# A gated recurrence with a binarized FFN: u in two single-pass parts, gates spread over two sweeps, signs on ScalarE, W_out of block 0 inside the second sweep

## The reference

```python
u = x @ W_in + b_in
g = sigmoid(x @ W_gate + b_gate)
h_t = tanh(h_prev @ A + u_t @ Bm)          # step by step, h0 = 0
y_t = h_t @ C.T + u_t @ D.T
y_t = g_t * y_t + (1 - g_t) * x_t
x = layernorm(x + (ys @ W_out + b_out + x))
bw = mean(abs(w), axis=1) * sign(w)        # of w1 and of w2
h = gelu(x @ bw1.T + b1)                   # exact gelu
out = layernorm(x + (h @ bw2.T + b2))
```

## Time and profile before

| | us |
|---|---|
| median of 3 runs (lowest to highest) | 439.53 (438.86 to 439.70) |
| the profiled execution, its own time | 438.74 |
| its span, first to last instruction | 436.9 |
| TensorE matmul busy | 422.2 (97%) |
| VectorE busy | 361.3 (83%) |
| ScalarE busy | 309.8 (71%) |
| GpSimd busy | 305.9 (70%) |

### The profile page before, as it was taken

How to read it: one execution, slowest core, us unless ns; L and a number is a source line. 1 busy time by engine, 2 the same in 40 slices (tenths; PEclk the granted TensorE clock), 3 DMA queues, 4 the chain that set the end, 5 groups by cost and what they waited for, 6 DMA issues and landing times.

```text
span 436.9 us, 8056 instructions
## 1 busy us (share of the span) xinstructions
PE 422.2 (97%) x2691; PEld 305.2 (70%) x2691; DVE 361.3 (83%) x788; ACT 309.8 (71%) x570; POOL 305.9 (70%) x304
## 2 busy tenths in 40 slices
PE   7999999999999999999999999999999999999982
PEld 4787887777756777676776867768677676766651
DVE  2666777766466899999999999999999999998574
ACT  1222224655547878889898898988989889797781
POOL 5199722255479977797977979779797797673523
PEclk9999999999999999999999999999999999999997
DMA  7954460000110113435153451434514245151422
GB/s 226 360 151 133 141 144 2 2 0 2 48 51 0 50 48 50 78 69 98 48 98 115 71 108 48 98 104 56 132 48 98 96 54 143 48 98 49 50 98 96
DMA packets 43895, 37.17 MB, mean 85 GB/s; under 512 B 35505, under 2 KB 37297, under 8 KB 43857
## 3 DMA queue, kind: packets, MB, share of 16 engines
q1 hardware_dynamic: 42528, 35.66, 33.6%
q0 software_dynamic: 272, 0.66, 0.6%
q10 hardware_dynamic: 1056, 0.36, 0.3%
HBM read 19.90 MB, written 8.39 MB: 65 GB/s over the span
## 4 chain that ended last, share of the span: by engine, by line
PE 72%; DVE 16%; ACT 4%; issue 4%; DMA 1%; SPq 0%; POOL 0%; POOLq 0%; DVEq 0%; ACTq 0%
PE bank L1049 17%; PE bank L1037 14%; PE bank L925 10%; PE bank L881 8%; PE bank L793 7%; DVE hid L1393 7%; PE bank L786 6%; PE bank L896 3%; PE bank L867 3%; ACT hid L644 3%; PE bank L778 3%; DVE gT L1406 3%; DVE bank L1376 3%; DVE bank L1399 2%; DVE gT L1388 2%
## 5 line engine op out<-in xcount | busy, mean ns | idle before, releaser
L1037 PE MATMUL bank<-xT,w1s 128*128 128x512 f16 x512 | 126.9, 380 | 2.4 <-DVE hid L1393 1.7
L1049 PE MATMUL bank<-w2s,hid 128*128 128x256 f16 x1024 | 125.3, 273 | 0.9 <-DVE gT L1406 0.8
L1049 PEld LDWEIGHTS bank<-w2s,hid 128*128 128x128 f16 x1024 | 98.6, 98 | 31.4 <-issue 5.6
L636 ACT ACTIVATE bank<-bank,b_col,alpha 128x512 f32<-128x512 f32 x128 | 96.8, 756 | 15.3 <-PE bank L1037 14.9
L1393 DVE SCALAR_TENSOR_TENSOR hid<-bank,small,hid 128x512 f16<-128x512 f32 x128 | 94.6, 740 | 14.9 <-ACT hid L644 14.9
L644 ACT ACTIVATE hid<-bank,small 128x512 f16<-128x512 f32 x128 | 86.6, 692 | 19.0 <-PE bank L1049 17.8
L1037 PEld LDWEIGHTS bank<-xT,w1s 128*128 128x128 f16 x512 | 46.0, 98 | 48.0 <-DVE hid L1393 7.1
L410 POOL TENSOR_TENSOR ys_lo<-gT,ys_hi 128x512 fp32r<-128x512 f32 x30 | 38.3, 1278 | 24.8 <-ACT ys_hi L609 24.8
L793 PE MATMUL bank<-hu,w_rec 128*128 128x128 f32 x208 | 45.5, 300 | 1.1 <-DVE hu L1156 0.9
L405 POOL TENSOR_TENSOR gT<-gT,xT 128x512 f32<-128x512 f32 x30 | 38.3, 1276 | 11.2 <-DVE gT L1279 11.0
L426 POOL TENSOR_TENSOR gT<-x_rows,b_row 128x1024 f32<-128x1024 f32 x16 | 38.0, 2378 | 9.6 <-DMA xT<-gT 9.6
(11 more groups left out here) (145 smaller groups left out, 807.7 us busy)
## 6 DMA issues: line engine op xcount, KB each, us to landing
x_load<-in_L_attn_x SPq DMA_DIRECT2D x16, 512.0 KB, 3.6
gT<-in_L_attn_x SPq DMA_DIRECT2D x15, 512.0 KB, 3.8
out_rows<-gT SPq DMA_DIRECT2D x15, 512.0 KB, 3.4
gT<-in_L_ffn_w SPq DMA_DIRECT2D x2, 1024.0 KB, 11.4
gT<-in_L_attn_x SPq DMA_DIRECT2D x4, 128.0 KB, 2.8
out_rows<-gT SPq DMA_DIRECT2D x2, 256.0 KB, 2.1
xT<-gT SPq DMA_TRANSPOSE x28, 4.1
w_gate<-in_L_attn_W_gate ACTq DMA_DIRECT2D x1, 256.0 KB, 7.6
```

The source lines that it names most:

```text
L636: nc.scalar.activation(bank[which][:, :], bank[which][:, :], ACT.Gelu, bias=b1_col[:, c:c + 1], scale=alpha1[:, c:c + 1]).then_inc(s_gelu, 1)
L1037: done = nc.tensor.matmul(bank[which][:, :], w1s[:, c, k, :], x1T[:, n, :, part, :, k, :], start=(k == 0 and part == 0), stop=(k == KD - 1 ...
L1049: done = nc.tensor.matmul(bank[tile // 2][:, tile % 2 * DM:(tile % 2 + 1) * DM], hid[:, c % 3, part, tile * P:(tile + 1) * P], w2s[:, :, c ...
```

## The change

1. **u from parts.** From the fourth block on (in load order, o >= WHOLE_U = 3), u is no longer a whole fp32 product. `w_pack` holds the low part of W_in in its left 64 columns and the high part in its right 64 (made by GpSimd at the start). VectorE casts x to its high part (`x_high`), GpSimd subtracts the low part, and `u_part` multiplies w_pack with the high part and then the low part. The right half of the result plus the left half is u: ScalarE copies the left half out (`u_copy`, into `u_rest`), and VectorE adds it in `u_out`.
2. **Transposes** of two steps share a bank, and `x_out` copies two steps at once.
3. **Gates** of five blocks (order `GATE_ORDER`, places 0 to 4) use the parts of x that u has needed and run as single pieces beside the steps from 12 on: one piece a step up to step 56, two up to 59, three from 60. 14 blocks have gates by parts (165 of their 168 pieces stand in the sweeps); two blocks (13 and 14 in x, places 14 and 15) have whole products in the tail.
4. **Signs** of w1 and w2 are made by ScalarE with the Sign function in eight quarters after the tanh of steps 28, 32, 34, 38, 40, 44, 46 and 50. w1 and w2 are loaded one block later.
5. **Block 0**: y in steps 86 and 90 in place of 90 and 96; W_out of block 0 in steps 97 to 100, in banks 4 and 5, no gate pieces in these six steps.
6. **Tail**: the order of GpSimd, ScalarE and VectorE is new around blocks 0 and 1, and `out_products(1, 0)` stands behind `y_products(2, 1)`.

```diff
+    WHOLE_U = 3
+    BEFORE = 5
+    IN_PARTS = NB - 2
+    GATE_ORDER = (9, 12, 15, 2, 5, 0, 1, 6, 7, 8, 3, 4, 10, 11, 13, 14)
+    FIRST_Y = (WARM + 11 * STEPS + 2, WARM + 12 * STEPS + 2)
+    FIRST_OUT = WARM + L - 7
+    def pieces_at(t):
+        if t < WHOLE_U * STEPS or t in FIRST_Y or FIRST_OUT <= t < FIRST_OUT + STEPS:
+            return 0
+        return 1 if turned_at(t)[0] < NB + 1 and t < NB * STEPS - 7 else 2 if t < NB * STEPS - STEPS else 3
...
+            pool.wait_ge(s_win, 16)
+            pool.tensor_copy(w_pack[:, :, NS:P], w_in[:, :, NS:P]).then_inc(s_wp, 1)
+            pool.wait_ge(s_wp, 1)
+            pool.tensor_tensor(w_pack[:, :, 0:NS], w_in[:, :, NS:P], w_pack[:, :, NS:P].bitcast(F32),
+                               ALU.subtract).then_inc(s_wp, 1)
...
-            for i, (stage, negative, sign) in enumerate(((w1_stage, neg_w1, w1_sgn), (w2_stage, neg_w2, w2_sgn))):
-                pool.wait_ge(s_w12, 32)
-                pool.tensor_scalar(negative, stage, 0.0, None, ALU.is_lt).then_inc(s_neg, 1)
-                pool.tensor_scalar(sign, stage, 0.0, None, ALU.is_gt).then_inc(s_neg, 1)
-                pool.wait_ge(s_neg, i * 2 + 2)
-                pool.tensor_tensor(sign, sign, negative, ALU.subtract).then_inc(s_sgn, 1)
+            for o in range(WHOLE_U, NB):
+                high, low = parts_of(o)
+                j = (B0 + o) % NB
+                for half in range(2):
+                    at = slice(half * (N // 2), (half + 1) * (N // 2))
+                    pool.wait_ge(s_xph, (o - WHOLE_U) * 2 + half + 1)
+                    pool.tensor_tensor(low[:, :, at], xT[:, j, :, at], high[:, :, at].bitcast(F32),
+                                       ALU.subtract).then_inc(s_xpl, 1)
...
             hu_low(1, 0)
-            hu_low(1, 1)
             first_rstd(0, 0)
             pool.wait_ge(s_rs1, 1)
+            hu_low(1, 1)
+            first_rstd(0, 1)
+            mix(1, 0)
+            pool.wait_ge(s_ys, KD + 1)
             hu_low(2, 0)
-            mix(1, 0)
-            first_rstd(0, 1)
-            pool.wait_ge(s_rs1, 2)
+            mix(1, 1)
+            pool.wait_ge(s_ys, KD + 2)
             hu_low(2, 1)
-            mix(1, 1)
...
+            def u_copy(o, half):
+                act.wait_ge(s_umm, o * 2 + half + 1)
+                act.wait_ge(s_u, o * 2 + half)
+                nc.scalar.activation(u_rest[NS:P, :], bank[4 + half][0:NS, 0:N // 2], ACT.Copy).then_inc(s_uc, 1)
...
+            SIGN_STEPS = (28, 32, 34, 38, 40, 44, 46, 50)
+            for t in range(WARM + L):
...
+                if s % 2 == 1 and WHOLE_U <= o + 1 < NB:
+                    u_copy(o + 1, s // 2)
+                if t in SIGN_STEPS:
+                    sign_quarter(*divmod(SIGN_STEPS.index(t), 4))
+                for g in range(NB * KD):
+                    if gate_half_done(g) + 1 == t:
+                        gate(g // KD, g % KD)
...
+            gate(14, 0)
             act.wait_ge(s_done, 1)
             hu_high(1, 0)
             hu_high(1, 1)
-            gate(GATED, 1)
-            gate(GATED + 1, 0)
-            gate(GATED + 1, 1)
+            gate(14, 1)
+            gate(15, 0)
+            gate(15, 1)
+            nc.scalar.activation(small[0:1, 29:30], ident[0:1, 0:1], ACT.Gelu)
+            act.wait_ge(s_scale, 1)
             hu_high(2, 0)
             hu_high(2, 1)
...
             ys_high(1, 0)
-            gate(GATED + 3, 0)
+            x1_hi(0, 0)
             ys_high(1, 1)
-            gate(GATED + 3, 1)
-            x1_hi(0, 0)
-            gate(GATED + 4, 0)
             x1_hi(0, 1)
...
+            def u_part(o, half, part):
+                pe.wait_ge((s_xph, s_xpl)[part], (o - WHOLE_U) * 2 + half + 1)
+                for k in range(KD):
+                    done = nc.tensor.matmul(bank[4 + half][:, 0:N // 2], w_pack[:, k, :],
+                                            parts_of(o)[part][:, k, half * (N // 2):(half + 1) * (N // 2)],
+                                            start=(part == 0 and k == 0), stop=(part == 1 and k == KD - 1))
...
+            for t in range(WARM + L):
+                o, s = divmod(t, STEPS)
+                if s % 2 == 0 and o < NB:
+                    pe.wait_ge(s_u, o * 2 + s // 2 + 1)
+                pe.wait_ge(s_h, t + 1)
+                scan_step(T0 + t if t < WARM else t - WARM, s % 2, s_scan)
+                if t < 2 * STEPS:
+                    opening(t)
+                elif o + 1 < NB:
+                    if t == 2 * STEPS:
+                        pe.wait_ge(s_wp, 2)
+                    u_part(o + 1, s // 2, s % 2)
+                    if o + 2 < NB:
+                        transpose_step(o + 2, s)
+                if t == WHOLE_U * STEPS:
+                    pe.wait_ge(s_wgs, 2)
+                for i in range(pieces_before(t), pieces_before(t + 1)):
+                    gate_piece(i)
+                if t // STEPS == NB - B0 + PREP:
+                    prepare_rows(s)
+                for m in range(KD):
+                    if t == FIRST_Y[m]:
+                        y_products(0, m)
+                if FIRST_OUT <= t < FIRST_OUT + STEPS:
+                    if t == FIRST_OUT:
+                        pe.wait_ge(s_ylo, KD)
+                    out_of(0, t - FIRST_OUT)
...
+            for i in range(pieces_before(WARM + L), IN_PARTS * KD * 6):
+                gate_piece(i)
+            gate_half(14, 0)
             pe.wait_ge(s_cmp, 3)
+            nc.tensor.matmul(bank[2][0:1, 0:1], gap_flag, ones[0:NS, 0:1], start=True, stop=True).then_inc(s_cnt, 1)
+            gate_half(14, 1)
...
+            gate_half(15, 0)
+            gate_half(15, 1)
             y_products(1, 0)
             y_products(1, 1)
...
             hidden(0, 0)
             hidden(0, 1)
             y_products(2, 1)
+            out_products(1, 0)
             out_products(1, 1)
             hidden(0, 2)
             ffn_out(0, 0)
...
+            def gate_x_hi(place):
+                slot = place % 2
+                if place > BEFORE:
+                    dve.wait_ge(s_gmm, (place - 1) * KD)
+                nc.vector.tensor_copy(xg_hi[:, slot, :, :], xT[:, GATE_ORDER[place], :, :]).then_inc(s_xgh[slot], 1)
...
-            gate_x_hi(7)
+            gate_x_hi(11)
             first_y_high(0)
             first_y_high(1)
-            gate_x_lo(7)
+            gate_x_lo(11)
...
             less_x(0, 0)
-            gate_x_hi(9)
+            gate_x_hi(13)
             first_gate(0)
-            gate_x_lo(9)
-            gate_x_hi(10)
+            gate_x_lo(13)
             first_mix(0)
             less_x(0, 1)
             first_gate(1)
             first_high(0)
             first_mix(1)
-            gate_x_hi(11)
-            gate_x_lo(11)
             first_high(1)
...
             first_sum(0, 0)
-            first_sum(0, 1)
             first_spread(0, 0)
             first_moments(0, 0)
+            first_sum(0, 1)
             first_spread(0, 1)
+            first_moments(0, 1)
             less_x(1, 0)
-            less_x(1, 1)
             gate_y(1, 0)
-            first_moments(0, 1)
-            gate_y(1, 1)
             first_norm(0, 0)
             first_norm(0, 1)
+            less_x(1, 1)
+            gate_y(1, 1)
             x1_lo(0, 0)
+            x1_lo(0, 1)
             less_x(2, 0)
-            x1_lo(0, 1)
             gate_y(2, 0)
             first_sum(1, 0)
```

More of the change, by code:

```diff
@@ new lines, in _ @@
+                if s % 2 == 1 and WHOLE_U <= o + 1 < NB:
[5 more added lines that the diff above has]
+                        gate(g // KD, g % KD)
+            for g in range(NB * KD):
+                if gate_half_done(g) + 1 >= WARM + L and g < IN_PARTS * KD:
+                    gate(g // KD, g % KD)
@@ L1183, in gate_x_lo @@
                                         ALU.subtract).then_inc(s_xgl[1], KD)
[L1185 removed]
+            x_out(0, 0)
             dve.wait_ge(s_bin, 16)
[L1187 to L1193 removed]
@@ L1194, in _ @@
-            heads(NB - B0, 0)
-            rest(NB - B0, 0, NB - 1)
-            heads(NB - B0 + 1, 1)
-            for j in range(1, B0):
-                rest(NB - B0 + j, j, j - 1)
-                if j + 1 < B0:
-                    heads(NB - B0 + j + 1, j + 1)
-                if j in (2, 3):
-                    gate_x_hi(j - 2)
-            u_out(NB - 1, B0 - 1, 1)
-            gate_x_lo(1)
+            u_out(0, 0)
+            x_out(0, 1)
+            u_out(0, 1)
+            x_out(1, 0)
@@ new lines, in _ @@
+            x_out(1, 1)
+            u_out(1, 0)
+            x_out(2, 0)
+            u_out(1, 1)
+            x_out(2, 1)
+            x_out(3, 0)
+            u_out(2, 0)
+            x_high(3, 0)
+            x_out(3, 1)
+            u_out(2, 1)
+            x_high(3, 1)
+            for o in range(2, NB - 1):
+                if o >= WHOLE_U:
+                    u_out(o, 1)
+                    x_out(o + 1, 1)
+                    x_high(o + 1, 1)
+                if o + 2 < NB:
```

(4 more changed lines are left out.)

470 lines of the change are left out of this document (219 added, 251 removed).

## The result

The changed kernel takes 445.59 us (median of 4 runs, 444.34 to 446.11), the kernel before 439.43 in the runs beside it: a ratio of 1.0137 [1.0111, 1.0163], 6.2 us slower. The forecast was +2.4 us (441.9). The sign was right, the size was not; 445.59 lies at the very edge of the range of 437.2 to 445.6.

A forecast was written before the change was run, and what follows sets the result against it. The loop's latency bounds the first sweep, TensorE alone the tail. 0.9 + 0.7 - 1.85 + 1.7 + 3.9 - 2.9 = +2.4 us on a median of 439.53 makes 441.9 us, range 437.2 to 445.6.

The forecast's parts named there:

- The sign: Whole kernel: slower, chance 0.60, against 0.26 for faster and 0.14 for the same; forecast +2.4 us.
- Wait at step 97: Second sweep: W_out of block 0 waits for both low parts of y, +3.9 us (2.5 to 4.3).
- rival (d): Step 97 and tail gaps: TensorE's clock falls; one fall about 2 us, 443.9; both gaps some 446; chance 0.12.
- Wait at step 86: Second sweep: y(0, 0), moved from step 90, waits for its inputs, +1.7 us (0.8 to 2.5).
- The gain beside it: Second sweep: step 60 loses its u products, two steps with y lose three gate products each, -1.85 us.
- Opening: Steps 0 to 7: steps 2, 4 and 8 wait for u's halves, +0.9 us (0 to +2).
- Steps 8 to 59: First sweep: u in parts through more engines, 0.98 to 0.985 a step, +0.7 us (-1.1 to +3.6).
- Rival (b): Recurrence: without fp32 passes for u the loop falls to 0.92 us a step, 437.1 us; chance 0.12.
- the prediction's own sign of being wrong: Recurrence: one of two waits missing, the step's period moved by over 0.05, or a tail under 20 us.
- Tail: After the last scan: hidden(0, 0) at 19.2, hidden(0, 2) at 24.6 for 28.95, then 1.45 lost; -2.9 us.
- No cost of the signs: First sweep: ScalarE's sign quarters fit behind a tanh and cost nothing.
- Rival (e): ScalarE: Sign is outside the Tanh and Sigmoid table set, 8 quarters add 20.5 us, 462; chance 0.02.

The follow-up runs named there:

- e1_order: Changed kernel with VectorE's gate_x_hi(13) and gate_x_lo(13) moved behind first_high(1): 439.20 us, ratio 0.9991 to the kernel before.
- e2_busy: Changed kernel with unused TensorE products, 30 ahead of the wait in step 97 and 24 ahead of y(2, 0) in the tail: 441.83 us, ratio 1.0062.
- e4_ylate: Changed kernel with y of block 0 in steps 88 and 90 instead of 86 and 90: 442.86 us, ratio 1.0091 to the kernel before.
- e7_unroll: Kernel before the change with only ScalarE's three loops over the recurrence's blocks written out: 433.83 us, ratio 0.9877.
- c2_filled: c1_orders with 18 unused products on TensorE ahead of hidden(0, 0): 433.52 us, ratio 0.9876 to the kernel before.
- c1_orders: Changed kernel with gate_x(13), u_out, block 0's y, and the tail's x1_hi(0, 1) and y(2, 0) reordered: 433.68 us, ratio 0.9877.

## Why the prediction was right or wrong

**The sign** was right for the reasons given: two new waits and a longer first sweep, together more than the gains. The wait in step 97 is the largest of them, and e1_order shows it: without it the loss is gone. The size was not right: +6.2 us for +2.4.

**Wait at step 97** (3.9): place, releaser and chain as forecast; 4.1 of it is wait. The 7.6 to 8.0 us from step 93 came out as 7.9. What the term lacked is that the steps in front had become shorter (0.92 for 0.95), so TensorE asked earlier, and the clock behind it.

**The clock** is the step that failed most. The sum assumed a granted clock of 1.00 across a wait that it had itself put at 3.9 us, and another gap in the tail, and gave the falls to rival (d) with 0.12, for one fall at about 2 us and both at "some 446". Both came, and the result is 445.59. Measured, the one in the sweep costs 1.6 us and the one in the tail about 1.9 (27.08 against e2_busy's 25.17, which still has a short one), 3.5 of the 3.8 us that the forecast was short. With the gaps filled, e2_busy is 2.7 us slower than the kernel before, close to the forecast's 2.4. That closeness is in part luck: its first sweep is 1.4 longer than forecast, its second sweep 0.7 shorter (+3.1 for +3.75), and hidden(1, 0) comes 2.7 sooner for 2.9. The "some 446" of (d) leans on the same luck. A forecast that rests on such a wait has the fall in its likeliest case.

**Wait at step 86** (1.7): 1.76, and e4_ylate's second sweep is shorter by just that. The gain beside it (-1.85; its terms add to 1.82) came out as 1.8: 0.34 in step 60 and 0.72 in each of the two steps with y.

**Opening** (+0.9): +1.14 with the later first scan, +0.4 without it. In the bounds.

**Steps 8 to 59** (+0.7): +2.1. The loop of u's parts was named and sized rightly (4.0 a block, 4.06 measured). The sum then took only +0.3 from it, where its own 4.0 for 3.9 a block is already 1.1 over 11 blocks. And 4.06 - 3.90 = 0.16 a block, over the 11 blocks of steps 12 to 55, is 1.8 us; step 58 adds 0.9 (1.80 long) where 0.4 was forecast; steps 8 to 11, at 0.90 each, give 0.3 back, and the others outside the loop the rest. The +2.1 is itself the difference of two larger terms: against e7_unroll, whose steps have the same tanh, the first sweep of the changed kernel is 5.7 longer (52.80 for 47.11), and the loops written out hide 3.6 of it.

**The step's own period** was the hidden term, and it fell out of the forecast altogether. Rival (b) had steps of 0.92, with the wrong cause: it put them down to u without fp32 passes. e7_unroll has fp32 u beside every scan and shorter steps still. The change writes ScalarE's loops out, which the diff shows and the prediction passed over; ScalarE's queue was not read for what stands between two tanhs. The 0.92 that rival (b) took from the earlier trace rows was a step outside the loops, and the 0.96 that was held against it one inside; the two differ in that, and both have three gate products beside them. In the second sweep the shorter step is worth about 1.0 us (43.01 for 44.00 in e7_unroll), which hid as much of the loss. It also met the prediction's own sign of being wrong, a period moved by over 0.05: most steps of the first sweep went from 0.95 and 1.01 to 0.92.

**Tail** (-2.9, hidden(0, 2) at 24.6): hidden(0, 0) came at 19.7 for 19.2, so the chain was read rightly. hidden(0, 2) came at 27.1 for 24.6: 0.5 of that is hidden(0, 0), and some 1.9 is TensorE's work from y(2, 0) to 143.57, at the low clock. With the clock at 1.00, and the first product moved forward, c2_filled has it at 24.5. Of the gain up to hidden(0, 2), 1.1 was lost again up to hidden(1, 0); 1.45 was forecast.

**No cost of the signs**: right. Rival (e) is false: a sign quarter takes 0.62 us on ScalarE with tanh and sigmoid around it and no table load, and the steps that hold one take 0.92.

**What the change is worth.** Both kernels measured here at 433.7 and 433.8 are reached in different ways. Measured against e7_unroll, which has the same form of ScalarE's program, the change as it stood costs some 11.5 us (2.6% by the ratios); with its orders mended it costs nothing and brings nothing. By stages, c1_orders takes 3.6 more in the first sweep than e7_unroll (50.72 against 47.11, the u loop at 3.87 a block), 1.9 less in the second (41.14 against 43.01) and 2.7 less up to hidden(1, 0) (40.97 against 43.64). Whether an order exists that keeps the 4.5 without the 3.6 stays open.

## What to carry to other kernels

Read the sequencer's rows of an engine that sits on a recurrence before anything else: writing out loops that had an instruction of 55 ns ahead of each of 96 dependent ones was worth 5.2 us, as much as the whole rebuilding of the work around it with every order mended. When work is moved ahead of a recurrence, look at what stands before it in every in-order queue: two operations for a later block cost 5.6 us, and moving them behind cost nothing. And a wait that you forecast at several us on TensorE must be priced with the lower clock behind it: here 1.6 us on top of 4.1.
